# A vision tower on one core: layer 2's experts as sorted tiles, with three smaller edits beside them

## The reference, cut to what matters

```python
x1  = mla(rmsnorm(x, w_ln1)) + x                  # latent attention
xn2 = rmsnorm(x1, w_ln2)
scores = sigmoid(xn2 @ W_router + routing_bias)   # 7 routed experts
top2 of the scores per token, weights divided by their sum
shared = (silu(xn2 @ Wg_s) * (xn2 @ Wu_s)) @ Wd_s # every token
routed = sum over the 2 chosen e: weight * (silu(xn2 @ Wg_r[e]) * (xn2 @ Wu_r[e])) @ Wd_r[e]
out = h + x1 + shared + routed
```

## Time and profile before

| | us |
|---|---|
| three executions | 876.67, 877.49, 879.45 |
| the profiled execution | 880.2 |
| its span | 878.6 |
| layer 0's experts, block | 143.5 to 305.5 |
| layer 1's experts, block | 357.0 to 471.2 |
| layer 2's experts, block | 614.5 to 709.5 |

### The profile page before, as it was taken

One profiled execution on the slowest core, in us unless ns is written; L12 is line 12 of the kernel. 1 busy time (PEld: TensorE's weight loads), 2 busy tenths in 40 slices (PEclk: granted clock), 3 DMA queues, 4 the chain that ended last, 5 costly groups with the idle time before them and its releaser, 6 DMA issues. The chain is left out here.

```text
span 878.6 us, 15379 instructions
## 1 busy us (share of the span) xinstructions
PE 714.9 (81%) x5469; PEld 622.0 (71%) x5469; DVE 414.8 (47%) x1111; ACT 240.2 (27%) x606; POOL 349.8 (40%) x410
## 2 busy tenths in 40 slices
PE   4597764799999768689987775786999976779997
PEld 3475653688888557689985563565999954469997
DVE  5835857644443344611104565484554446651211
ACT  2131310145554022123311330051544314311110
POOL 1226631456663030144313423521577458425211
PEclk9889975699999886699997896886899987969999
DMA  9102104578874550677622300300122512065703
GB/s 366 58 0 45 16 1 139 179 243 251 252 251 135 183 172 1 222 238 234 214 86 78 29 3 17 38 6 1 43 102 72 191 37 22 2 228 167 292 24 99
DMA packets 72665, 104.04 MB, mean 118 GB/s; under 512 B 43701, under 2 KB 55381, under 8 KB 70677
## 3 DMA queue, kind: packets, MB, share of 16 engines
q1 hardware_dynamic: 63013, 81.88, 29.6%
q0 software_dynamic: 6432, 16.00, 6.0%
q10 hardware_dynamic: 3152, 5.26, 1.6%
HBM read 89.27 MB, written 13.84 MB: 117 GB/s over the span
## 5 line engine op out<-in xcount | busy, mean ns | idle before, releaser
L2223 PEld LDWEIGHTS ps<-l0e_xg_fm,l0e_ring 128*128 128x128 f32 x544 | 63.6, 191 | 12.8 <-issue 12.5
L2223 PE MATMUL ps<-l0e_xg_fm,l0e_ring 128*128 128x128 f32 x544 | 68.5, 279 | 1.8 <-issue 0.9
L301 POOL TENSOR_TENSOR norm_r<-norm_ve,const_sb 128x2 f32<-128x2 f32 (+1 forms) x30 | 21.0, 699 | 116.1 <-DVE norm_ve L294 88.1
L868 PE MATMUL ps<-x_fm,w_sb 128*128 128x296 f32 x208 | 54.2, 413 | 0.0
L2223 PE MATMUL ps<-l1e_xg_fm,l1e_ring 128*128 128x128 f32 (+1 forms) x408 | 49.7, 280 | 1.1 <-ACT l1e_xg_fm L2270 0.6
L2223 PEld LDWEIGHTS ps<-l1e_xg_fm,l1e_ring 128*128 128x128 f32 (+1 forms) x408 | 48.8, 187 | 2.3 <-issue 1.5
L868 PEld LDWEIGHTS ps<-x_fm,w_sb 128*128 128x128 f32 x208 | 39.4, 190 | 11.6
L2123 POOL DMA_INDIRECT l0e_xg_tm<-x_scratch,l0e_rows_u x34 | 33.1, 972 | 30.9 <-PE ps L2199 24.1
L359 PE MATMUL ps<-const_sb,xn 128*128 128x128 f32 x70 | 16.1, 360 | 35.5 <-DVE xn L328 35.3
L2138 POOL DMA_INDIRECT l0e_y_scratch<-l0e_y_tm,l0e_rows_u x34 | 33.5, 986 | 24.7 <-ACT l0e_y_tm L2307 24.7
L396 PE MATMUL ps<-const_sb 128*128 128x128 f32 x284 | 42.1, 318 | 0.0
(11 more groups left out here) (463 smaller groups left out, 1802.4 us busy)
## 6 DMA issues: line engine op xcount, KB each, us to landing
l0e_ring<-in_l_experts SPq DMA_DIRECT2D x34, 514.0 KB, 5.4
l1e_ring<-in_l_experts SPq DMA_DIRECT2D x17, 704.0 KB, 5.6
expert_w<-in_l_experts SPq DMA_DIRECT2D x4, 2048.0 KB, 8.0
l_more_w<-in_l_experts SPq DMA_DIRECT2D x4, 2048.0 KB, 8.7
expert_w<-in_l_experts SPq DMA_DIRECT2D x8, 768.0 KB, 4.3
l0e_down_w<-in_l_experts SPq DMA_DIRECT2D x1, 4096.0 KB, 15.2
l1e_down_w<-in_l_experts SPq DMA_DIRECT2D x1, 3072.0 KB, 11.8
w_sb<-in_weights SPq DMA_DIRECT2D x2, 1032.0 KB, 13.3
```

What stands on the lines that cost most here:

```text
L868: mm = pe.matmul(ps[:, slot * (2 if both else 1) + b, 0:HALF], w, src[:, c0:c0 + HALF], start=(k == 0), stop=(k == len(part) - 1))
L2223: mm = pe.matmul(ps[0:widths[m], which, m * P:(m + 1) * P], ring[:, n % RING, c:c + widths[m]], xg_fm[:, n % 2, k, :], start=(k == 0), sto ...
```

## The change

1. Layer 2 uses `tiled_experts` with the 7 routed experts and a new argument `dense`. The shared expert's five tiles (`S` = 5) run first in the same loop, straight from `x_fm`; the steps of the routing are put between them on PE and DVE. Then come 16 sorted tiles. The gathered rows are scaled by `w_ln2` as they are copied (two ACT copies a tile). `experts`, `router_of` and `first_split` go. All of layer 2's down matrices and the shared expert's weights come into `expert_w` at the end of layer 0 (`fetch_l2`, 2.6 MB where 1.6 MB were fetched); layer 3's weights (4 MB) are fetched after layer 2's last tile.
2. In all three tiled layers `turn(n + 1)` stands between gate and up, and ACT's `copy_x` comes first in its round.
3. `pool.drain()` behind GpSimd's last scatter.
4. Layer 0: the first of the four slots is no longer multiplied on PE but multiplied and added by DVE.
5. `stay_awake(34)` ahead of the norm in `tokens`, `stay_awake(26)` in the `project_out` of layer 0 and of layer 2's first attention.

The diff, cut to its core:

```diff
@@ tokens, project_out
+                        stay_awake(pe, 34)
                         tensor(pe)
...
+                        if two:
+                            stay_awake(pe, 26)
                         tensor(pe)
@@ tiled_experts
+            S, first = (0, 0) if dense is None else (TILES, 1)
+            source = xn if source is None else source
...
+                slots = range(1, top) if many else range(top)
...
                         bring_back(sp, range(0, TILES, 2))
-                        if following is not None:
-                            name, next_width = following
-                            for u in range(2):
-                                fetch(sp, name, next_width, u, u)
+                        if then is not None:
+                            then(sp)
...
                                                         y_tm[:, e % YS, :], None).then_inc(s_y[e % YS], 16)
+                        pool.drain()
                         gpsimd(pool)
...
-                        for n in range(NT + 1):
-                            if n < NT:
-                                whose[n % 2] = pe.value_load(tile_e[n:n + 1, 0:1])
-                                pe.wait_ge(s_ring[n % RING], 16 * (n // RING + 1))
-                                pe.wait_ge(s_xfm, n + 1)
+                        for n in range(S + NT + 1):
+                            r = n - S
+                            if n < S:
+                                w_n, x_n = dense_w, x_fm[:, :, n * P:(n + 1) * P]
+                            elif r < NT:
+                                whose[r % 2] = pe.value_load(tile_e[r:r + 1, 0:1])
+                                pe.wait_ge(s_ring[r % RING], 16 * (r // RING + 1))
+                                pe.wait_ge(s_xfm, x_steps * (r + 1))
+                                w_n, x_n = ring[:, r % RING, :], xg_fm[:, r % 2, :, :]
...
                                     mm.then_inc(s_made, 1)
-                            if n + 1 < NT:
-                                turn(n + 1)
+                                    if which == 0 and 0 < r + 1 < NT:
+                                        turn(r + 1)
                             if down_b is not None:
                                 down_bias(n)
+                            if S and n == 1:
+                                count_chosen()
+                            if S and n == 3:
+                                list_rows()
...
+                            if S and r + 1 == 0:
+                                pe.wait_ge(s_expert, 1)
+                                turn(0)
...
-                            for i in range(top):
+                            for i in slots:
...
+                            for k in range(KT):
+                                act.activation(xg_fm[:, n % 2, k, :], ps[:, 2 + n % 2, k * P:(k + 1) * P], ACT.Copy,
+                                               scale=col(x_scale, k)).then_inc(s_xfm, 1)
...
+                        for n in range(S + NT + 1):
+                            r = n - S
+                            if 0 <= r + 1 < NT and not (S and r < 0):
+                                copy_x(r + 1)
...
-                            if n + 1 < NT:
-                                copy_x(n + 1)
...
+                            if many:
+                                for t in range(*GROUPS[g]):
+                                    x = h[0:real[t], t, :]
+                                    dve.wait_ge(s_back[t], 16)
+                                    signal(dve.scalar_tensor_tensor(out=x, in0=back[0:real[t], 0, t, :],
+                                                                    scalar=share[0:real[t], 0, t:t + 1], in1=x,
+                                                                    op0=ALU.mult, op1=ALU.add))
+                                wait()
                             dve.wait_ge(s_sum, g + 1)
@@ build
+        def fetch_l2(sp):
+            sp.dma_start(dense_w, a["l2_experts"][0, :, :]).then_inc(s_w[0], 16)
+            sp.dma_start(down_l2, a["l2_experts"][1:, :, down_at:l0_width].rearrange("e p n -> p e n"))\
+                .then_inc(s_w[1], 16)
...
-            experts("l2e", "l2_experts", L2_E, 2, gates, ...
+        tiled_experts("l2e", "l2_experts", L2_E - 1, 2, (P, P), weight("mla_router"), row("mla_rb", L2_E - 1),
+                      dense=(dense_w, s_w[0], 16, down_l2, s_w[1], 16, xn, "w_ln2"), source=x0n, then=fetch_l3)
```

More of the change, by code:

```diff
@@ L273, in build, with stay_awake @@
         done = {"norms": 0, "chain": 0}
+        def stay_awake(pe, count):
+            for _ in range(count):
+                pe.matmul(ps[:, 1, 0:P], ident, ident, start=True, stop=True)
         GROUPS = ((0, 2), (2, 4), (4, TILES))
@@ L388, in _ @@
                     scalar(act)
-        def stay_awake(pe, count):
-            for _ in range(count):
-                pe.matmul(ps[:, 1, 0:P], ident, ident, start=True, stop=True)
         def load(sp, layer):
@@ L1628, in first_split @@
-        def first_split(tag, mt, where, clipped=False):
-            up = 2 * KT * mt * P
-            up_hi, up_lo = (sb(f"{tag}_up0_{n}", [P, up], F32R, where=where) for n in ("hi", "lo"))
-            bias_sb = sb(f"{tag}_bias_sb", [P, 2, L0_BIASES], where=where) if clipped else None
-            s_whi, s_wlo, s_bias = (sem(f"{tag}_{n}", where) for n in ("whi", "wlo", "bias"))
-            ready = (1 + fetched[0]) * 16
-            def high(act):
-                act.wait_ge(s_w[0], ready)
-                act.activation(up_hi[:, :], expert_w[:, 0, 0:up], ACT.Copy).then_inc(s_whi, 1)
-                if clipped:
-                    at = up + mt * D
-                    act.activation(bias_sb[:, 0, :], expert_w[:, 0, at:at + L0_BIASES], ACT.Copy).then_inc(s_bias, 1)
-            def low(pool):
-                pool.wait_ge(s_whi, 1)
-                pool.tensor_tensor(up_lo[:, :], expert_w[:, 0, 0:up], up_hi[:, :].bitcast(F32), ALU.subtract)\
-                    .then_inc(s_wlo, 1)
-            return up_hi, up_lo, bias_sb, s_whi, s_wlo, s_bias, high, low
@@ L2016, in tiled_experts @@
                 tile_e = sb(f"{tag}_tile_e", [NT, 1], U32, where=st)
-                down_w = sb(f"{tag}_down_w", [P, E, MT * D], where=st)
+                if dense is None:
+                    down_w, s_dw, down_ready = sb(f"{tag}_down_w", [P, E, MT * D], where=st), sem(f"{tag}_dw", st), 16
+                else:
+                    dense_w, s_dense, dense_ready, down_w, s_dw, down_ready, residual, x_scale = dense
+                    y_dense = sb(f"{tag}_y_dense", [P, S, D], where=st)
+                    s_fold, s_base = sem(f"{tag}_fold", st), sem(f"{tag}_base", st)
                 at_e = sb(f"{tag}_at_e", [P, TILES, E], where=st)
@@ L2159, in _ @@
-                        mm.then_inc(s_cnt, 1)
-                        stay_awake(pe, 10)
-                        pe.wait_ge(s_marks, 2)
-                        for j, (i, t) in enumerate(pairs):
-                            pe.wait_ge(s_hits, i + 1)
-                            mm = pe.matmul(ps[:, 7, 0:2 * NT], hits[0:real[t], i, t, :],
-                                           marks[0:real[t], j, :, :].rearrange("p c n -> p (c n)"),
-                                           start=(j == 0), stop=(j == len(pairs) - 1))
@@ new lines, in list_rows @@
+                        def list_rows():
+                            pe.wait_ge(s_marks, 2)
+                            for j, (i, t) in enumerate(pairs):
+                                pe.wait_ge(s_hits, i + 1)
+                                mm = pe.matmul(ps[:, 7, 0:2 * NT], hits[0:real[t], i, t, :],
+                                               marks[0:real[t], j, :, :].rearrange("p c n -> p (c n)"),
+                                               start=(j == 0), stop=(j == len(pairs) - 1))
+                            mm.then_inc(s_sums, 1)
@@ L2260, in _ @@
                             act.activation(tables[:, i, :], const(table), ACT.Copy).then_inc(s_tables, 1)
+                        if dense is not None:
+                            act.preload_act_table(ACT.Sigmoid)
                         act.wait_ge(s_raw, 1)
-                        act.activation(probs[:, :, :], probs[:, :, :], ACT.Exp).then_inc(s_exp, 1)
+                        act.activation(probs[:, :, :], probs[:, :, :], ACT.Exp if dense is None else ACT.Sigmoid)\
+                            .then_inc(s_exp, 1)
                         act.preload_act_table(ACT.Silu)
@@ L2391, in by_limit @@
                                                           a=1), ALU.mult))
+                        if dense is not None:
+                            dve.sem_inc(s_raw, 1)
+                            dve.wait_ge(s_exp, 1)
                         if many:
@@ L2919, in build @@
             project_out("mlao", ctx_fm, "mla_o", None, xn, (xn, x0n, True, "w_ln2"))
-            gates = sb("l2_gates", [P, TILES, L2_E], where=st)
```

(8 more changed lines are left out.)

598 lines of the change are left out of this document (130 added, 468 removed).

## The result

In the comparison on which the forecast is judged the changed kernel took **849.03 us** (847.91 to 850.18, 4 runs), the kernel before 877.08 (872.88 to 879.45, 4 runs): ratio 0.9703, 95% interval 0.9663 to 0.9743. The forecast was 862.6, in a range of 853 to 871. The direction was right, and the gain was nearly twice what I summed: 28.0 us, against 14.9. Runs more than 1.5% above the fastest of the same kernel count as slow: they are left out of the ratios, and the medians of the later comparisons are over all runs.

A forecast was written before the change was run, and what follows sets the result against it. PE was taken to bound the sorted-tile loops and layer 2's experts, no engine the whole. Terms -5.3 - 5.3 - 1.2 - 3.1 = -14.9 gave 865.3 us profiled, 862.6 as median; range 853 to 871.

The forecast's parts named there:

- The turn: Layer 0's sorted tiles: transposes behind gate and an earlier copy end a wait of 0.165 us in 32 tiles, -5.3 us.
- The drain's 4.2 and 1.1: Ends of layer 0's and 1's blocks: POOL's drain hidden behind the last scatter, -4.2 and -1.1 us.
- The closing sum: Layer 0's closing sum: five of 20 PE matmuls go, DVE gets five operations, -1.2 us.
- The new matmuls: Keep-awake matmuls in `tokens` and `project_out`: fit into PE's waits and buy little, 0 us, bounds -7.8 and +0.5.
- the signs: Expected in the profile: layer 0's tiles 2.95 us apart, 1.4 us gaps, layer 2's block 92 us, clock 0.50 at three starts.
- Rivals B: Layer 2 gives nothing: first tile 4 us later, tiles at 3.11, +6.6 us, total 869; chance 0.15.
- C: Block ends: the drain does not move, 4.2 and 1.1 us stay and layer 2 adds 1.0, total 868.9; chance 0.08.
- D: Layer 2's sorted tiles not PE-bound, period up to 4.17 us, +19.5, total 882.1; slower from 3.88 on; chance 0.03.
- From the last down to the block's end as in layer 1, 20.4: Layer 2's block: its tail was taken to last 20.4 us, part of the block's -3.1 us.
- Layer 2's first tile at B + 23.7, period 2.95: Layer 2's block, starting at B: first sorted tile 23.7 us in, 16 tiles at 2.95 us, block -3.1 us.
- The copy in layer 1 is hidden: 0: Layer 1's sorted tiles: no wait for the copy there, so turning earlier gives 0 us.
- Rival A: The new matmuls hold PE's clock up into the next block: -7.8 us more, total 854.8; chance 0.12.

The follow-up runs named there:

- y_drain0: The changed kernel without GpSimd's drain behind the last scatter, on a slow chip: 879.53 us, ratio 0.9944 to the kernel before.
- y_slot0: The changed kernel with layer 0's first choice summed on PE again and none of DVE's five new operations, slow chip: 874.00 us, ratio 0.9921.
- x_no_awake: The changed kernel without the 34 and 26 new keep-awake matmuls: 872.26 us, ratio 0.9874 to the kernel before.
- w_more_only: The kernel of w_more without the change's own 34 and 26 keep-awake matmuls: 843.11 us, ratio 0.9665 to the kernel before.
- x_b_awake: The kernel before with nothing but the 34 and 26 new keep-awake matmuls added: 880.50 us, ratio 0.9997.
- z_before: The kernel before, unchanged, run for its trace on a slow chip: 880.21 us.
- z_more: The changed kernel with 6, 6 and 4 more keep-awake matmuls amid the transposes of every norm: 865.58 us, ratio 0.9822 to the kernel before.
- v_more: The kernel of w_more once more, beside the changed kernel (870.49 us) on one slow chip: 864.90 us, ratio 0.9791 to the kernel before.
- w_more: The changed kernel with 3, 3 and 2 keep-awake matmuls amid the transposes of every norm, quick chip: 843.04 us, ratio 0.9673 to the kernel before.
- y_after: The changed kernel again, unchanged, as yardstick on a slow chip: 870.99 us, ratio 0.9892 to the kernel before.

## Why the prediction was wrong

Right: layer 0's block on the quick chip, as a sum (10.9 us for 10.7), though not by each of its terms. The turn gave 6.2 us from the first transposes to the last down, for 5.3: the period fell by 0.24, not 0.165. My 1.86 us for gate and up was taken behind a wait; without it they take 0.89 + 0.89, so the tile is 2.87 and not 2.95. The drain's 4.2 and 1.1 are confirmed by y_drain0. The closing sum gave 0.5 us in the pair, for 1.2, and 0.1 to 0.6 by y_slot0. The new matmuls are worth nothing in x_no_awake and w_more_only, as priced. Of the signs, the tiles, the three gaps and layer 2's first tile were near; the clock was at the half level as layer 0's projection and logits started, but not for layer 2's latent products (ten records in 2.40 us). Rivals B, C and D fell on both kinds of chip: layer 2's block is 8.5 us shorter on the quick one and about 6 on the slow ones, the gaps moved, and the sorted tiles of layer 2 are 2.87 and about 3.2 us apart, under the 3.88 of D.

Wrong, in order of size, against 14.9 us:

- *"From the last down to the block's end as in layer 1, 20.4"*, and layer 1's closing priced at the drain alone. The 20.4 us were no normal closing: they held a late scatter (1.6) and a half-clock sum (1.6), and the granted clock of 0.88 stood in the very row that I took them from. Layer 1 gained 3.2 us more, and layer 2, whose tail I copied from it, has 18.77 from the last down to the next block where I had 20.4 + 1.4: 3.0 more. That is 6.2 us from one misread stage.
- *Nothing between the blocks.* Layer 1's output projection to its block takes 12.9 to 13.0 us in the kernel before (two traces) and in x_b_awake, and 10.2 to 10.4 in every kernel that has at least two of layer 0's edits and no new matmuls in the norm: 2.7 us, with the projection at the full clock. Which edit does it was not separated, and why stays open. Layer 2's attention gave 4.4 us in the profiled pair, which is one execution's clock, as z_before shows.
- *Layer 2's first tile at B + 23.7, period 2.95.* The first tile's gate came at B + 22.2, 1.5 us earlier (the counts took 0.7 us of PE, where I had 1.4), and from there to the end of the last down it was 46.9 us, not 47.8: 2.4 more in all.
- *The copy in layer 1 is hidden: 0.* Its steady tiles were no faster, but the stage from first transposes to last down was shorter by 0.75 us, in its first tiles.

Without layer 2's attention these make 12 us (6.2 + 2.7 + 2.4 + 0.75), and with its 4.4 they make 16.5 of the 17.3 us by which the profiled pair beat the sum. The medians' gain is 13.1 over the sum. The mechanisms that I priced held on the quick chip; what failed was the reference, since I took a stage of one trace as the undisturbed case. And I set the range as if chips were alike: on the slow kind the gain is 8.6 to 13.4 us, and there 14.9 is too much, since the tiles of layer 0 go from 3.17 to about 3.24 us in the mean and not to 2.87. The time lies 4 us under my range on one kind of chip and at its upper end or above on the other (870.5 to 872.8).

Rival A was refused on the ground that only transposes stand in front of the blocks. That was the right reading of the earlier trace rows, and z_more and v_more show its other half: with products amid the transposes the clock holds. Its price was wrong, though: the ten latent records took 4.11 us in all at the half clock and take 2.40 at the full one, so they could save 1.7 us and not 4.1, and the rival's sum was 5.4 us and not 7.8.

## What to carry to other kernels

Before a stage's length is used as the price of another stage, look for what disturbed it: a code fetch among the packets of the transfer that ends it, and a granted clock under 1.00 in its row. Count a wait on the last scatter from its issue to the return that waits for it, and compare it with the other layers. When only transposes precede a block, two or three small products between them can hold the clock (5.6 us here, on one chip), if they fit into the wait even at the half clock: six of them cost 3.6 us in one stage. And try a change on more than one chip: an edit that took 0.24 us off each tile on one took nothing that shows on the three others.

## What the runs showed of the hardware

- A drain of GpSimd behind the last scatter cost nothing that shows beside the closing sum; left to the block's end (y_drain0 beside y_after) it costs 4.3 us after 68 indirect DMAs, 1.1 after 34 and 1.0 after 32.
- A fetch of code (0.02 MB) among the 96 packets of a scatter goes with a late landing: 2.39 to 2.47 us from issue to return without one, 2.41 to 4.44 with one. One and the same program has it in one execution and not in another (layer 2 of w_more and v_more, 4.44 and 2.40).
- PE idle for 2.2 us ahead of a sum left the clock full once (w_more, layer 2, 4.56 us) and found it at the half level another time (the kernel before, layer 1, 6.17 us).
- The changed kernel takes 849 us on one chip and 870 to 873 on others, with the sorted tiles of layers 0 and 2 at 2.87 or about 3.2 us, and layer 1's tiles at 4.17 on both. What holds them there the profile does not show.
